# Held-back key stores, turned rows inside key work, grouped feed-forward work and moved first matrices in a one-core attention and expert kernel

## The reference, cut to what matters

```
x = x + L0_xattn(layernorm(x), ctx, mask)     # one-head attention over the context
x = x + L0_ffn(layernorm(x))                  # 4 rounds: xt = prob * silu(xt @ W1[e]) @ W2[e],
                                              #   e = argmax of softmax(xt @ router[round]), 16 experts
x = x + L1_xattn(layernorm(x), ctx)           # 16 heads of 8
x = x + L1_ffn(layernorm(x))                  # sigmoid(xr @ Wr) * (relu(xk @ Wk)**2 @ Wv), token shift
x = x + L2_xattn(layernorm(x), ctx, keymask)  # 16 heads, masked keys
x = x + L2_ffn(layernorm(x))                  # 64 experts, top 8, and 2 shared ones
x = x + L3_xattn(layernorm(x), ctx)           # 16 heads, queries and keys RMS-normalized per head
x = x + L3_ffn(layernorm(x))                  # 8 experts, top 2, with a capacity
```

## Time and profile before

| what | value |
|---|---|
| median of 3 timed runs | 2349.59 us (2340.85 to 2354.88) |
| the profiled execution | 2356.95 us, span 2355.2 us |
| PE busy | 2115.2 us, 90% of the span |
| ACT, DVE, POOL busy | 1449.9, 1307.6, 234.8 us |
| mean granted clock of PE | 0.936 |
| DMA | 352.81 MB, 150 GB/s on average |

### The profile page before, as it was taken

One profiled execution on the slowest core, in us unless ns is written; L12 is line 12 of the kernel. 1 busy time (PEld: TensorE's weight loads), 2 busy tenths in 40 slices (PEclk: granted clock), 3 DMA queues, 4 the chain that ended last, 5 costly groups with the idle time before them and its releaser, 6 DMA issues. The chain is left out here.

```text
span 2355.2 us, 42618 instructions
## 1 busy us (share of the span) xinstructions
PE 2115.2 (90%) x16862; PEld 1384.8 (59%) x16862; DVE 1307.6 (56%) x1796; ACT 1449.9 (62%) x1808; POOL 234.8 (10%) x305
## 2 busy tenths in 40 slices
PE   5877989989989689999948999997988999996999
PEld 3554755846748456666635666664655666664554
DVE  4553344343343576667558777755457766643333
ACT  2334456455464478888827888884428888884341
POOL 1006033041240310000000000001010000000000
PEclk9997998989989889999968999997989999997999
DMA  5858446355464487887318788732027778832000
GB/s 196 235 178 316 159 171 236 118 191 197 151 228 152 141 201 183 196 183 185 94 35 199 185 185 197 181 83 66 1 45 187 184 184 195 185 79 73 0 8 7
DMA packets 119756, 352.81 MB, mean 150 GB/s; under 512 B 20160, under 2 KB 54846, under 8 KB 118942
## 3 DMA queue, kind: packets, MB, share of 16 engines
q1 hardware_dynamic: 105774, 322.41, 50.3%
q0 software_dynamic: 13776, 27.54, 3.8%
HBM read 257.58 MB, written 91.23 MB: 148 GB/s over the span
## 5 line engine op out<-in xcount | busy, mean ns | idle before, releaser
L964 ACT ACTIVATE a_probs<-a_score 128x1200 f32<-128x1200 f32 x768 | 857.7, 1169 | 149.3 <-PE a_score L875 149.3
L875 PE MATMUL a_score<-a_qstack,a_kstack 128*128 128x400 f32 x2304 | 551.7, 372 | 9.8 <-DVE a_kstack L1025 7.7
L875 PEld LDWEIGHTS a_score<-a_qstack,a_kstack 128*128 128x128 f32 x2304 | 379.5, 190 | 179.8 <-issue 129.5
L837 PE MATMUL a_numer<-a_probs,a_v 128*18 128x200 f32 (+1 forms) x9216 | 471.6, 335 | 0.0
L837 PEld LDWEIGHTS a_numer<-a_probs,a_v 128*18 128x18 f32 (+1 forms) x9216 | 229.0, 97 | 184.0 <-issue 88.5
L1025 DVE TENSOR_TENSOR a_kstack<-a_kraw,a_kstack 64x2888 fp32r<-64x2888 f32 x96 | 303.8, 3164 | 5.1 <-ACT a_kstack L931 1.8
L1020 DVE CAST a_kstack<-a_kraw 128x2888 fp32r<-128x2888 f32 x90 | 149.8, 1665 | 12.8 <-DVE a_own L1081 9.0
L1033 DVE TENSOR_TENSOR a_qstack<-a_qrep,k_groupmask 128x1600 fp32r<-128x1600 f32 x48 | 87.5, 1824 | 121.7 <-PE a_score L875 121.2
L1680 PEld LDWEIGHTS f0r_ph<-f0r_xsT,f0r_w 128*128 128x128 f32 x896 | 119.4, 199 | 30.6 <-issue 12.5
L1680 PE MATMUL f0r_ph<-f0r_xsT,f0r_w 128*128 128x128 f32 x896 | 123.5, 283 | 9.2 <-DVE f0r_xsT L1868 9.2
L2080 ACT ACTIVATE f_hidden<-f_ph,f_b 128x400 f32<-128x400 f32 x128 | 75.8, 593 | 88.6 <-PE f_ph L2004 80.8
(11 more groups left out here) (358 smaller groups left out, 2725.1 us busy)
## 6 DMA issues: line engine op xcount, KB each, us to landing
a_kraw<-keys SPq DMA_DIRECT2D x384, 361.0 KB, 7.0
values<-kv_vst SPq DMA_DIRECT2D x32, 1296.0 KB, 5.2
a_v<-values SPq DMA_DIRECT2D x48, 864.0 KB, 5.8
keys<-kv_made SPq DMA_DIRECT2D x48, 722.0 KB, 5.2
l0a_ctxT<-in_ctxT SPq DMA_DIRECT2D x16, 722.0 KB, 7.8
kv_ctxT<-in_ctxT SPq DMA_DIRECT2D x16, 722.0 KB, 8.5
l0a_ctx<-in_ctx SPq DMA_DIRECT2D x16, 704.0 KB
l0a_mask<-in_mask_BxSxS_ik SPq DMA_DIRECT2D x16, 564.1 KB
```

Source lines behind the costliest of these rows:

```text
L837: last = pe.matmul(numer[32 * g:32 * g + PC, p * 2 * SQ:(p + 1) * 2 * SQ], v[0:rows(t), j, t, (2 * g + p) * PC:(2 * g + p + 1) * PC], prob ...
L875: last = pe.matmul(to, kstack[:, j, g * SK + t * 128:g * SK + (t + 1) * 128], qstack[:, j, g * GH:(g + 1) * GH, :], start=True, stop=not s ...
L964: act.activation(probs[:, n % NP, :].rearrange("p (g q) -> p g q", g=SPAN), slot_ps[:, n % 2, :, 0:GQ], ACT.Exp, scale=HSCALE).then_inc(ex ...
```

## The change

- `KeyMaker.RING` is 5, with a fifth `k_out`. `load_context(b)` waits itself until batch b - 2 has kept all its keys. ACT's `raw` no longer waits for `n_full` of the batch before.
- SP in a round: early batches store layers 1 and 3, load the next context, then store layer 2. Of the late batches only the first one's layer 1 is stored at once; the first context waits for `fetched[1]`, and the other five stores and the second context wait for `fetched[3]`. In the last round nothing is held back.
- PE and DVE in a round: the first `turn` goes into the second early batch's keys ahead of x = 4; DVE does `weigh(0)` and the first `turned_in` before that batch's normals, and its peaks behind the blocks. PE's wait for all banks of the early keys becomes a wait in each of the first two `up` and `down` and values.
- Round tails: `turn_back(0)` goes ahead of x = 4 of the last batch's keys, `route(0)` and `turn_back(1)` ahead of x = 8; ACT copies the turned rows within its key work; DVE interleaves `scale`, `normals` and `pick`.
- The 16 first matrices of `L0_ffn` are issued at the end of `l0_attention`'s SP program.
- The flag becomes `unsafe`, one DVE operation more, and the two bodies change places in both `If`s.
- `l1_ffn` works by groups from the start, ACT does the multiplications by mu, and relu and sigmoid alternate under one table. `l2_ffn`'s picker is one ACT copy from `ident2`, made in `setup` by one DVE addition. `l3_ffn` loads two experts in its layernorm and the other six at the start of its own block.

```diff
-    RING = 4
+    RING = 5
     def load_context(self, sp, b):
+        if b >= 2:
+            sp.wait_ge(self.k_kept, 6 * (b - 2) + 6)
...
# l0_attention, sync
+            for e in range(E0):
+                sp.dma_start(m.w1[:, e, :], ins["L0_W1"][e]).then_inc(m.up_in, 16)
...
# l0_round, sync
-            if layer == 0:
-                for e in range(E0):
-                    sp.dma_start(m.w1[:, e, :], ins["L0_W1"][e]).then_inc(m.up_in, 16)
-            for pair in (early, late):
-                for b in pair:
-                    maker.values_sp(sp, b)
-                for b in pair:
-                    maker.keys_sp(sp, b)
-                    if b == early[1]:
-                        sp.wait_ge(xs_in[GROUPED - 1], 16)
-                    if b + 2 < B:
-                        maker.load_context(sp, b + 2)
+            for b in early:
+                maker.values_sp(sp, b)
+            for b in early:
+                maker.keys_sp(sp, b, (1, 3))
+                if b == early[1]:
+                    sp.wait_ge(xs_in[GROUPED - 1], 16)
+                maker.load_context(sp, b + 2)
+                maker.keys_sp(sp, b, (2,))
+            for b in late:
+                maker.values_sp(sp, b)
+            if more:
+                maker.keys_sp(sp, late[0], (1,))
+                sp.wait_ge(fetched[1], 16 * BG)
+                maker.load_context(sp, late[0] + 2)
+                sp.wait_ge(fetched[TG - 1], 16 * BG)
+                maker.keys_sp(sp, late[0], (3, 2))
+                maker.load_context(sp, late[1] + 2)
+                maker.keys_sp(sp, late[1], (1, 3, 2))
+            else:
+                for b in late:
+                    maker.keys_sp(sp, b, (1, 3, 2))
...
# l0_round, tensor
-            for b in early:
-                keys(b)
-            for x in range(6):
-                maker.keys_freed(pe, late[0], x)
+            keys(early[0])
+            keys(early[1], {FIRST_TURN: [lambda: turn(0)]})
...
             def up(s, j):
                 pe.wait_ge(w1_ready, s + 1)
-                pe.wait_ge(silued, s + 1)
+                if s < C:
+                    maker.keys_freed(pe, late[0], s)
+                else:
+                    pe.wait_ge(silued, s + 1)
...
             keys(late[0])
             if more:
-                turn_back(0)
-            keys(late[1])
...
-            if more:
-                route(0)
-                turn_back(1)
+                keys(late[1], {4: [lambda: turn_back(0)], 8: [lambda: route(0), lambda: turn_back(1)]})
+                route(1)
                 turn_back(2)
-                route(1)
                 route(2)
                 turn_back(3)
                 route(3)
+            else:
+                keys(late[1])
...
# l0_round, vector
-            for b in early:
-                maker.normals_dve(dve, b, banks)
-                for n in (1, 2):
-                    maker.largest_dve(dve, b, n)
+            maker.normals_dve(dve, early[0], banks)
+            for n in (1, 2):
+                maker.largest_dve(dve, early[0], n)
             weigh(0, 0)
             turned_in(0)
+            maker.normals_dve(dve, early[1], banks)
             groups(dve, group)
+            for n in (1, 2):
+                maker.largest_dve(dve, early[1], n)
...
-            maker.normals_dve(dve, late[1], banks)
-            scale(1)
-            scale(2)
             if more:
+                maker.normals_dve(dve, late[1], banks, (0,))
+                scale(1)
+                maker.normals_dve(dve, late[1], banks, (1, 2))
                 pick(0)
+                scale(2)
+                pick(1)
+                pick(2)
                 scale(3)
-                for g in range(1, TG):
-                    pick(g)
+                pick(3)
...
# heads_attention, tensor and vector alike
-            flag = pe.value_load(safe[0:1, 0:1], min_val=0, max_val=1)
+            flag = pe.value_load(unsafe[0:1, 0:1], min_val=0, max_val=1)
             with pe.If(flag):
-                batches(False)
-            with pe.Else():
                 batches(True)
+            with pe.Else():
+                batches(False)
...
# heads_attention, vector
-            dve.tensor_scalar(safe[:, :], bound[:, 0:1], SAFE / HSCALE, None, ALU.is_lt).then_inc(flag_ready, 1)
+            steps.done(dve.tensor_scalar(bound[:, 1:2], bound[:, 0:1], SAFE / HSCALE, -1.0, ALU.is_lt, ALU.mult))
+            dve.tensor_scalar(unsafe[:, :], bound[:, 1:2], 1.0, None, ALU.add).then_inc(flag_ready, 1)
...
# l1_ffn, vector: the new order (shift, square and add are of one group)
-            for n, t in ((1, xk), (0, xr)):
-                ch.done(dve.tensor_scalar(t[:, :, :], xn, mu[:, n:n + 1], None, ALU.mult))
-                ch.done(dve.scalar_tensor_tensor(t[:, :, 1:SQ], xn[:, :, 0:SQ - 1], mu[:, 2 + n:3 + n],
-                                                 t[:, :, 1:SQ], ALU.mult, ALU.add))
+            shift(xk, 1, 0, xk_ready)
+            shift(xr, 0, 0, xr_ready)
+            shift(xk, 1, 1, xk_ready)
+            square(0)
+            shift(xr, 0, 1, xr_ready)
+            shift(xk, 1, 2, xk_ready)
+            square(1)
+            shift(xr, 0, 2, xr_ready)
+            add(0)
...
# l2_ffn, scalar
             act.preload_act_table(ACT.Exp)
+            act.copy(picker[:, :, :].rearrange("p c (j f) -> p (c j) f", f=H2),
+                     k.ident2[:, :].unsqueeze(2).to_broadcast([128, E2, H2])).then_inc(picker_made, 1)
...
# l3_ffn
-            for e in range(E3):
+            load_experts(sp, range(2))
...
         @block.sync
         def _(sp):
+            load_experts(sp, range(2, E3))
```

181 lines of the change are left out of this document (108 added, 73 removed).

## The result

The changed kernel takes 2318.37 us in the median of four runs (2316.3 to 2322.36), the kernel before 2349.95 beside it (2340.85 to 2354.88): ratio 0.9872, 95% interval 0.9838 to 0.9906. It is 31.6 us faster where 58.6 were forecast, and 0.4 us outside the range (2272 to 2318).

The account below looks back on a forecast made before the run. PE, busy 90% of the span, was taken as the bound, leaving only its waits and standstills between scopes to win. Seven terms summed to 58.1 us: 2299 for the profiled execution, 7.4 above the median, so 2291; range 2272 to 2318.

Parts of the forecast that it names:

- The flag's sense: Attention branches: swapping the bodies moves the jump from end to head; 8.6 us won, 3.1 paid, 5.5 net, bounds 0 and 13.
- rival (b): Attention heads: the jump is exposed in full, 3 x 2.8 us more, 2299 us in all; chance 0.08.
- First matrices: Round 1: expert matrices issued in the first attention shorten ACT's wait for a value store; 9.5 us gain, bounds 4 and 12.
- 10.5 earlier PE reaches it at 224.5 and waits to 229: Round 1, first turn inside the second batch's keys: PE arrives 10.5 us earlier, then waits for the first gathered block.
- Block starts: Expert block starts of the other three rounds: first down matmul earlier, 4.5 us each, 13.5 in all.
- so the first down matmul is at 554.0: Block start: ACT's table at 552.70, plus 0.6 turn and 0.60 Silu, puts down at 554.0 instead of 559.32.
- Tails: Ends of three rounds: last pick at 659.3 against 663.80, 4.5 us each, 13.5 in all.
- DVE has done picks 0 to 2 before it: Round tail: the first three picks are finished before the last gathered rows land at 653.6.
- rival (c): Held-back stores and contexts spill into the next round; tails and block starts win nothing net, 27 us lost, 2318; chance 0.07.
- 12.9 us of cover: Next round's start: twelve value tiles precede its first store, 12.9 us after SP's first issue in round 1, covering moved stores.
- Rival (a): Rounds give half, every moved wait being replaced in part; 13.5 us lost, 2305; chance 0.21.
- three signs of being wrong: ACT's value-store waits growing in rounds 2 to 4; PE waiting over 2 us at the turn; first score matmuls over 2 us later.

Follow-up runs that it names:

- e1: The changed kernel with the flag's sense as before, the usual body standing first again: 2313.05 us, ratio 0.9840 to the kernel before.
- e12: The changed kernel without the attention's second body and its branch, the flag still loaded: 2303.65 us, ratio 0.9817 to the kernel before.
- e2: The changed kernel with the first turn behind the second batch's keys in round 1 only: 2308.97 us, ratio 0.9817 to the kernel before.
- e3: The changed kernel with PE in l2_ffn waiting first for the up weights and biases only, the rest later: 2316.56 us, ratio 0.9852 to the kernel before.
- second, fourth and fifth set: Three of five sets of runs, each on its own chip beside the kernel before, whose medians there were 2369.6, 2366.1 and 2366.5 us.
- e7: The changed kernel with the tail's order on PE, ACT and DVE as before, stores still held back: 2344.21 us, ratio 0.9875 to the kernel before.
- first and third set: Two of five sets of runs, both on one chip beside the kernel before, whose medians there were 2353.5 and 2351.7 us.
- e5: The changed kernel unaltered, run again in the second set: 2348.8 us, ratio 0.9900 to the kernel before.

## Why the prediction was wrong, by its steps

*Bound and direction*: right; PE is the busy engine, and every part but the flag won in sum, if mostly less than forecast.

*The flag's sense* failed most: forecast +5.5, measured -4.3 (+10.6 at the ends, -14.9 at the heads), confirmed by e1 and e12. I took the end's branch of 3.77 us as the price at the head, and a cover of 2.8 us. The jump there takes 7.41 us. (0.9 and 0.2 us at three heads are 3.3 us and not the 3.1 that I charged; it changes nothing.) That the head would pay was rival (b), with a chance of 0.08 and, with what the forecast had charged already, 3.8 us a head; it was 5.0. My lower bound of 0 rested on a head that costs no more than the tail, for which no row spoke. It is 10 us of the miss.

*First matrices*: +9.5 forecast, +1.3 measured with the slower blocks. The step that failed is "10.5 earlier PE reaches it at 224.5 and waits to 229". PE came to the turn at 218.8 and stood 8.54 us (5.1 of the shift are the shorter attention); the stretch behind it, forecast at 10.3 us from the landing to the first down matmul, took 14.4, the keys at first at the lower level of the clock (granted 0.50 from 227.4 to 229.9; their pass of the bank average 1.92 us for two matmuls and not 1.02) and 2.0 us between Silu and down matmul, 1.36 of them a load of the block's expert number. I had the wait and the low clock, but not the alternative: e2 shows that with the turn behind the keys as before only 6.6 us follow it. So the early turn costs where the rows are not in; that it gains where they are was not shown. The scatter's landing slipped as well, 6.3 us from its last issue and not 2.3.

*Block starts*: 10.3 of 13.5. ACT ended as computed; the step "so the first down matmul is at 554.0" put nothing between the end of the Silu and the down matmul, though the earlier trace rows has 2.1 us there (557.18 to 559.32). Measured were 1.0 to 1.4 us, in which PE's sequencer waits for the Silu and loads the expert number. Round 4 had its wait for the landing, 1.26 us.

*Tails*: 10.2 of 13.5. Landing and POOL's floor were about as forecast; the step "DVE has done picks 0 to 2 before it" failed, the third pick ended at 633.43 and the last scaling began behind it. That the held-back stores have cover in the next round was right in the traces without stalls (18.2, 19.7 and 17.3 us from first value copy to first squares, before 18.6, 20.0 and 18.3), so rival (c) did not come. But the 12.9 us of cover that I read off the first round were SP's issues of the matrices: in round 4 the first value store is issued 8.0 us after the round's scan, 11.4 us after the last held-back store.

*l1_ffn*: 2.4 of 3.5; the stretch took 23.0 us where I had 21, perhaps by more waits between small groups than counted, which was not looked into. *l2_ffn*: the layernorm gave its 5.3 us to the tenth, and 3.1 went into the wait for weights; the step that failed was to stop at the layernorm and not to ask what lands when, since the loads start with it. e3 gives it back. *l3_ffn*: 7.9 for 7.3, right.

The sum of the terms is then 30.0 and not 58.1: of the 28 us missing the flag took 10, round 1 took 8, block starts, tails and l2_ffn 3 each and l1_ffn 1, and l3_ffn gave 0.6 more. The nearest rival in time is (c), with 2318 against 2318.37, and that is luck: its spill did not come, and the tails and block starts, which it has win nothing, won 20.5 us. Rival (a), half of the gain of the rounds (2305), has in its mechanism, a wait put where another was, what round 1 did; but the tails and block starts kept three quarters of theirs, so it is not the cause either. Of the three signs of being wrong two came: the turn inside the keys waited 8.54 us in round 1, and the first score matmuls came over 2 us later. The third came in part: ACT's waits for value stores (over 0.5 us each) sum to 3.1, 4.6 and 3.0 us in rounds 2 to 4, before 1.7, 4.9 and none, without longer value stretches.

## What to carry to other kernels

A far jump is not abolished by turning its condition round, it is moved; look for the place where an engine has slack longer than the jump, and take no price for it from another place. When a step is moved into a queue ahead of other work, the question is not how long it takes but how late its data can be: an early turn lost 5.6 us where its rows were not in, and an interleaved tail won 3.4 us with quick landings and lost 1.1 without. When a stage gets shorter, ask first which loads were started with it. And when an end is computed by adding durations, take the gaps between them from the rows as well: the 2.1 us between Silu and down matmul stood there.

## What the runs showed of the hardware

In the second, fourth and fifth set PE stopped handing on results for 2 to 9 us in much the same places: the interleaved tail, the last values and keys of a round. ACT's row there and the stretches around it, of the unaltered kernel in the fourth set (columns as in the earlier trace rows):

```profile
324.33 0.49 ACT L1837 COPY k_xnT<-f0r_pt 128x400 f32<-128x400 f32 x1 [5.79 <-remote]
...
318.00:320.00 2.00, 2.00 (x9) 1.09 (x8) 0.75 (x1) 0.54 (x2) 1.55 (x2) 1.00 0.88 358
320.00:322.00 2.00, 0.73 (x2) 0.00 (x0) 0.00 (x0) 0.00 (x0) 1.54 (x2) 1.00 0.16 38
322.00:324.00 2.00, 0.00 (x0) 0.00 (x0) 0.00 (x0) 0.00 (x0) 1.47 (x2) 1.00 0.16 41
324.00:326.00 2.00, 0.61 (x1) 0.50 (x2) 0.05 (x1) 1.56 (x3) 1.00 (x1) 0.82 0.18 45
```

PE's matmuls are recorded up to 320.7 at the full clock, the transposes that ACT waits for at 317.7 to 318.3; the signal comes at 324.3, from no instruction that the profile names, and after it the clock is at its lower level (0.50 granted from 326 to 328). The stops of 4.9 to 8.6 us are all of this kind, at turned rows inside the late keys; with the old order of the tail (e7) none is over 2.3 us. The kernel before has such a stop of 2.19 us in its tail in the last set:

```profile
337.00 0.61 ACT L597 ACTIVATE kv_klog<-f0r_pr,kv_eps 128x420 f32<-128x420 f32 x1 [2.19 <-remote]
```

In the first and third set, which are one chip, and in the two first traces none has one. The changed kernel was some 30 us slower on such chips in its median, before 13 to 20; on such a chip the old order of the tail had the lower median (2344.2 against 2348.8 us, e7 and e5, intervals overlapping) and tails 3.7 to 4.9 us shorter. The cause was not settled: three chips have the stops and one, with two sets on it, has none, and in the row shown PE had been busy at full clock before; nothing here tells more.
